# One repeating order in place of three: a software-pipelined kernel without order strings of its own for start and end

## The reference

```python
x = L0(x, theta, phi)                   # rotate pairs of the 256 columns by two angles of the sequence
# L1, expert chosen by the sequence: 256 -> 1024 -> 256, gelu between
y = layernorm(gelu(x @ Wi[e] + bi[e]) @ Wo[e] + bo[e] + x) * gamma[e] + beta[e]
# L2, one of three branches chosen by the sequence, two of them with two matmuls, the third with three
y = layernorm(y + branch_c(y)) * gamma + beta
# L3, conditioned transformer layer, 16 heads of 16
x = layernorm(y) * (1 + scale) + shift
q, k, v = x @ Wq + bq, x @ Wk + bk, x @ Wv + bv
p = softmax(q @ k.T / 4 + bias[b, h], masked)     # bias is 32 x 16 x 256 x 256
x = x + (p @ v) @ Wo + bo
h = layernorm(x) * g2 + beta2
out = x + gelu2(h @ W1 + b1) @ W2 + b2            # 256 -> 1024 -> 256
```

## Time and profile before

| | |
|---|---|
| median of 3 runs | 2104.13 us (2099.43 to 2105.55) |
| the profiled execution, its own time | 2105.55 us |
| span in its profile | 2103.8 us |
| mean granted TensorE clock | 0.985 |
| PE busy | 1934.4 us, 92% |
| DVE busy | 1591.0 us, 76% |
| ACT busy | 1377.0 us, 65%, of which 437.5 us are 341 table loads |
| DMA | 356 MB, mean 169 GB/s |

### The profile page before, as it was taken

The page is one execution under the profiler, slowest core; times in us unless marked ns, Lnnn a source line. Parts: engine busy times, 40 slices in busy tenths (PEclk is TensorE's granted clock), DMA queues, the critical chain, the costliest instruction groups (busy, mean ns, idle before and its releaser), DMA issues.

```text
span 2103.8 us, 43391 instructions
## 1 busy us (share of the span) xinstructions
PE 1934.4 (92%) x14131; PEld 1678.5 (80%) x14354; DVE 1591.0 (76%) x5373; ACT 1377.0 (65%) x2210; POOL 252.6 (12%) x361
## 2 busy tenths in 40 slices
PE   5789999999999999999999999999999999899786
PEld 4678888888888888888888888888888888788676
DVE  4567877777887788887777788777888877877764
ACT  3367677677667677767767767766676676666443
POOL 1111111011111011111101111101111110111100
PEclk9799999999999999999999999999999999999998
DMA  6656555665555465654555655556665545653350
GB/s 207 206 155 181 184 151 155 183 200 180 183 174 148 151 200 187 195 179 150 153 180 181 192 174 173 158 169 197 186 194 183 174 145 166 213 156 130 117 151 11
DMA packets 222311, 356.12 MB, mean 169 GB/s; under 512 B 29523, under 2 KB 120147, under 8 KB 222068
## 3 DMA queue, kind: packets, MB, share of 16 engines
q1 hardware_dynamic: 222068, 352.99, 54.7%
HBM read 294.12 MB, written 58.79 MB: 168 GB/s over the span
## 4 chain that ended last, share of the span: by engine, by line
PE 68%; DVE 20%; issue 7%; ACT 3%; DMA 1%; ACTq 0%; SPq 0%; POOL 0%; DVEq 0%; POOLq 0%
PE pD L471 44%; PE pX L687 12%; PE pS L471 10%; DVE bias_ring L1178 8%; DVE bias_ring L975 5%; PE pC L471 1%; PE pC L709 1%; DVE x_nat L972 1%; DVE crossed L972 1%; ACT L777 1%; ACT gelu_out L777 1%; ACT probs L777 1%; DMA out<-res 1%; ACT hid L777 1%; DVE y_nat L978 0%
## 5 line engine op out<-in xcount | busy, mean ns | idle before, releaser
L1178 DVE CUSTOM_DVE_ANT_0 bias_ring<-pS,bias_ring 128x256 f32<-128x256 f32 x1024 | 389.6, 418 | 221.8 <-PE pS L471 219.9
L777 ACT ACTIVATE probs<-pX 128x512 f32<-128x512 f32 x512 | 304.6, 595 | 249.8 <-PE pX L687 247.8
L777 ACT ACT_TABLE_LOAD x341 | 437.5, 1283 | 19.5 <-PE pD L471 12.0
L687 PE MATMUL pX<-ident,bias_ring 128*128 128x128 f32 x2048 | 326.8, 283 | 91.0 <-DVE bias_ring L975 73.8
L687 PEld LDWEIGHTS pX<-ident,bias_ring 128*128 128x128 f32 x2048 | 229.0, 142 | 191.2 <-DVE bias_ring L975 181.2
L975 DVE TENSOR_SCALAR bias_ring<-bias_ring,row_max 128x256 f32<-128x256 f32 x1024 | 321.4, 356 | 18.3
L471 PE MATMUL pS<-k_stack,q_stack 96*128 96x256 f32 x1024 | 305.1, 380 | 0.9 <-DMA k_stack<-k_spill 0.9
L471 PE MATMUL pD<-x,raw 128*128 128x256 f32 x1024 | 248.3, 386 | 1.8 <-ACT gelu_out L777 1.0
L471 PE MATMUL pD<-raw,gelu_out 128*128 128x256 f32 x1024 | 238.2, 380 | 0.0
L471 PEld LDWEIGHTS pS<-k_stack,q_stack 96*128 96x128 f32 x1024 | 198.3, 194 | 20.1
L471 PEld LDWEIGHTS pD<-x,raw 128*128 128x128 f32 x1024 | 189.3, 192 | 27.2 <-issue 4.1
(11 more groups left out here) (148 smaller groups left out, 3700.5 us busy)
## 6 DMA issues: line engine op xcount, KB each, us to landing
bias_ring<-in_fside SPq DMA_DIRECT2D x512, 256.0 KB, 4.2
raw<-in_experts SPq DMA_DIRECT2D x128, 512.0 KB, 4.6
q_spill<-hid SPq DMA_DIRECT2D x96, 256.0 KB, 3.4
k_spill<-hid SPq DMA_DIRECT2D x96, 256.0 KB, 3.4
q_stack<-q_spill SPq DMA_DIRECT2D x128, 192.0 KB, 4.0
k_stack<-k_spill SPq DMA_DIRECT2D x64, 384.0 KB, 5.6
norm<-in_expert_rows SPq DMA_DIRECT2D x32, 384.0 KB, 4.0
x_nat<-in_x SPq DMA_DIRECT2D x32, 256.0 KB, 3.3
```

The costliest lines, as they stand in the source:

```text
L687: last = e.transpose(pX[:, k, t * P:(t + 1) * P], bias_ring[:, u % NBIAS, t, k * P:(k + 1) * P], ident[:, :])
L777: return e.activation(o, i, func, bias=bias, scale=scale)
L1178: e.tensor_tensor_reduce(bias_ring[:, n, t, :], pS[:, t, :], bias_ring[:, n, t, :], 1.0, -3.4e38, ALU.add, ALU.max, row_max[:, n, t:t + 1] ...
```

## The change

FIRST and LAST go. The repeating string runs 36 times, and each engine leaves out the first letters of f, h and r, as many as SKIP says; letters of a stream that has ended do nothing.

```diff
-FIRST = {...}
-LAST = {...}
-OUTSIDE = 7
+SKIP = {"PE": (9, 101, 37), "ACT": (14, 56, 55), "DVE": (12, 53, 47), "POOL": (3, 0, 6), "SP": (10, 42, 4)}
...
+            skip = dict(zip("fhr", SKIP[engine]))
             next(extra, None)
-            for letter in FIRST[engine] + ORDER[engine] * (NB - OUTSIDE) + LAST[engine]:
-                next(streams[letter], None)
+            for _ in range(NB + 4):
+                for letter in ORDER[engine]:
+                    if skip.get(letter):
+                        skip[letter] -= 1
+                    else:
+                        next(streams[letter], None)
```

More of the change, by code:

```diff
@@ L30 @@
 MASKED = -2.0 ** 100
[L36 to L49, removed]
 ORDER = {
```

## The result

| | before | after |
|---|---|---|
| median | 2104.1 us (2099.43 to 2105.55) | 2119.64 us (2117.53 to 2122.37) |
| profiled execution, span in it | 2105.55, 2103.8 | 2116.27, 2114.5 |
| mean granted TensorE clock | 0.985 | 0.980 |

The changed kernel is slower: ratio 1.0079, 95% interval 1.0058 to 1.0099. The forecast was 2102.3, with a range to 2117. What these two traces show is therefore some two thirds of the loss; the traces of the experiments account for the rest (at the end of the account of the prediction).

The account below looks back on a forecast made before the run. PE was taken to bound the middle (busy 1481 of 1550.5 us), unchanged, but not the ends. Start +2.1 and end -3.9 gave -1.8 us: span 2102.0, or 2102.3 against the median 2104.1; range 2092 to 2117.

Parts of the forecast that it names:

- What does not change: Middle, repetitions 5 to 29: same order and distances as before, so its 1550.5 us stay.
- The start, g1's turn: Start: DVE's rotation, moved ahead of f0's first sum, ends at 56.4; PE turns at 58.2 without waiting, 2.3 us gained.
- The serial part: Start, ahead of h0: g1 ends at 78.3, then uncovered f0 and f1 steps; h0's first turn at 110.7, was 89.4.
- h0, 16 cycles ... 56.7: Start, h0's heads: 52.2 us by cycles, plus 3 for DVE's block and 1.5 for small waits, to 167.4.
- DVE has f1's sum and scaling between maxima 1 and 2, 3 us more: Start, inside h0: this DVE block adds 3 us to the cycles.
- The start's sum of +2.1: Whole start: its end comes at 259.6 us against 257.5, a loss of 2.1 us.
- Repetition 32: End, no g left: 51.2 us by cycles, +4.4 for DVE and +0.9 for clock, 56.5; old stretch 57.8.
- Repetition 33 ... 46.6 by cycles, 50.3 taken: End, r alone and f31 v: 46.6 us by cycles, 50.3 taken because the old 49.1 had exceeded its rule.
- The 23.0 and 36.4: Last stretches: h31 turn 7 to 15 takes 23.0 us (24.8 before), then r31 alone 36.4 (36.9 before).
- Bunched r steps and the clock: Slower rival at the end: bare cycles at half clock, ten to twelve, cost +10 us, 2112; chance 0.13.
- The serial start: Slower rival: f0 q, k, v and f1 lose g1's cover, up to +14 us at the start, 2114; chance 0.17.

Follow-up runs that it names:

- j: Kernel before with the repeating order at the end and extra unread transposes in bare cycles of the last 24 heads and r31's waits: 2103.03 us, 0.9996.
- l: Kernel before, old order throughout, with extra unread transposes in the last 24 heads and in r31's waits: 2107.76 us, ratio 1.0013.
- o: Changed kernel with f1's sum and scaling moved on DVE ahead of h0's maxima 0 and 1: 2119.56 us, ratio 1.0066.
- a: Changed kernel's new start with the old LAST at the end: 2117.75 us, ratio to before 1.0061.
- k: Changed kernel, order untouched, with the transposes of h at the start and of j at the end: 2109.55 us, ratio to before 1.0019.
- h: Changed kernel with 80 extra unread transposes on PE ahead of waits of f0 and f1: 2116.74 us, ratio to before 1.0054.
- b: Kernel before with old FIRST kept and the repeating order to the end: 2110.57 us, ratio 1.0023.
- d: Kernel before with all of g1 ahead of f0's q, k and v, then the old order and LAST: 2125.47 us, ratio 1.0099.
- i: Kernel before with 48 extra unread transposes ahead of the first matmul and 38 in f0's waits: 2103.4 us, ratio 0.9999.
- r: Old start with the transposes of i, repeating order at the end with those of j: 2100.79 us, ratio to before 0.9977.
- g: Kernel before with the repeating order until h30 turn 6, then the old order of what is left, no transposes: 2106.57 us, ratio 1.0007.

## Why the prediction was wrong, by its steps

- **What does not change** held: 1550.8 for 1550.5 us, and 31.3 and 60.8 for the 31.5 and 60.7 ahead of it. ACT has one table load more (342 for 341, 1.3 us each), which the prediction did not have.
- **The start, g1's turn**: 58.2 as forecast, but by luck. The rotation was done at 53.6 and not 56.4, because the input had landed by 51.4, and PE did not wait for it. PE itself came late, busy without a gap at half clock (a clock of 0.50 from 50 us on):

```profile
51.43 0.76 DVE L943 TENSOR_TENSOR crossed<-x_nat,rot_sin 128x256 f32<-128x256 f32 x2 [5.61 <-DMA x_nat<-in_x]
```

```profile
58.13 1.09 PE L442 MATMUL pD<-ident,x_nat 128*128 128x128 f32 x4
```

  In j and l, with the old start, g1 turn came at 58.2 and 58.1 as well, so the 2.3 us that were forecast as gained are inside what chance does there.
- **The serial part** was right: g1 done at about 79 (78.3), h0 turn 0 at 112.3 (110.7), and q_stack and k_stack did not hold it up.
- **"h0, 16 cycles ... 56.7"** is the step that failed at the start: 61.6. "DVE has f1's sum and scaling between maxima 1 and 2, 3 us more" was not what was short: it cost 2.1 (4.4 for 6.5 in o), and the three cycles with two g steps took 15.2 us for the 16.1 they were given. The nine cycles of 2.6 (turns 0, 4 to 8 and 12 to 14) took 28.5 us for 23.4: four were 2.6, the others 3.3 to 4.7. The three cycles of the deep branch took 4.4, 5.5 and 5.2, together 15.0 for 12.8. I priced cycles by PE's steps; DVE's and ACT's steps of the same sequences stand in some of them. For turn 5 that is DVE's scaling of g2, shown above; in turns 10 and 11 PE waits 1.4 us for DVE and 2.0 for ACT inside the deep branch, and these two cycles were there to be read in the trace of before (h0 turns 14 and 15, 5.4 and 5.2 us). These waits were read in the trace, not tried; the one block that was tried, in o, gave 2.1 us in its cycle and nothing in the time.
- **The start's sum of +2.1** was +8.5 in the trace, and 0.61%, 12.8 us, in a's time. By the ladder below, 8.8 us of the loss are order.
- **Repetition 32**: 56.7 for 56.5 in the kernel after, by luck: with the same order the eight other traces have 58.3 to 60.6, at clocks of 0.94 to 0.89 in place of 0.97.
- **"Repetition 33 ... 46.6 by cycles, 50.3 taken"** failed: 53.7, and 51.6 in j_end_warm and 51.3 in k with a clock of 0.97 and 1.00. **The 23.0 and 36.4** were 24.2 and 37.6; with transposes 23.1 and 33.9 in k. The sum was 297.7 for 291.9, and 300.9 to 301.9 in the three other traces of this end. The step that failed here is the clock: 0.9 us for it in repetition 32 and nothing in the three stretches behind. Over these stretches it is some 7 us that transposes take back, and up to 4 in repetition 32 that they do not.
- **Bunched r steps and the clock**, a rival at 0.13, is what happened at the end. It was priced at 10 us. The transposes took 7.2 us from h's median and 7.5 from b's (0.35% and 0.27% by the ratios, 7.4 and 5.7 us); in the traces of the end they took 7.7 and 7.2. The page TensorE: Matmul & The Clock Gate of the Trainium skill, cited there, agrees in kind: the clock over the last 37.6 us was 0.76.
- **The serial start**, a rival at 0.17, had its price nearly right (+10 to +14), but its point of decision, h0 turn 0 after 117, was wrong: it came at 112.3 and the loss was there. d shows the same from the other side.
- **The two rivals together** were not given a chance. With b's loss alone the kernel stays inside the range, with a's alone it is at its upper edge (2116.9 by the ratio); their sum, 2104.1 + 12.8 + 4.8 = 2121.7 by the ratios of a and b, does not.

The ladder, each step one edit: after 1.0079; transposes at the start 1.0054; and at the end 1.0019; the old order of the start 0.9977. In time that is 2119.6, 2116.7, 2109.6, 2100.8: 2.9 us clock at the start, 7.2 clock at the end, 8.8 the order of the start (the last rung also has i's 86 transposes there in place of h's 80). By the ratios the three steps are 5.3, 7.4 and 8.8 us, so the first is the least certain. The last rung lies under the kernel before, 2.2 us of it between j and r by transposes in the old start. That these gained nothing between before and i leaves open how much of it is the clock.

Why the medians of after and before differ by 4.8 us more than their traces can be read from the other traces. Up to h27 turn 7 six of them have the start of before, and they reach it between 1803.7 and 1809.0 us, on average at 1806.0; before, at 1808.0, is the second slowest. The two with the start of after reach it at 1816.8 (after) and 1815.9 (a): 10.3 us later on average, and not 8.8. From there on after was the fastest of the four traces of its end, whose mean is 300.6 us, against 296.2 for the five of the old end: 4.4, and not 1.9. Together that is 14.7 us, near the 15.5 of the medians. The profiled execution of before had a poor start, and that of after a good end.

## What to carry to other kernels

Price a reordered stretch on every engine, cycle by cycle: a cycle that is bare on PE may hold another engine's block, and work moved ahead of the heads is repaid only if the heads then get shorter. Where the steady order is cut off into a ramp, look at the granted clock of the ramp beside its idle time; here an end with cycles in which PE is busy 1.0 of 2.6 us lost some 7 us to the clock alone. Matmuls without use in such waits brought that back, and the same ones put into the old end, on top of its work, cost 3.6 us. And trace a kernel more than once before a stretch of a few microseconds is explained: one order's end varied by 4 us here.

## What the hardware showed that was not expected

- The same cycle of matmuls without a wait inside took 6.0 us at a clock of 0.53 and 3.7 at 1.00. A bare head cycle, PE's turn and scores and then DVE's maximum and subtraction, lost less: 3.4 us at 0.53 (h0 turn 0 before) and 2.6 at 1.00 (after).
- The tail of one chain, r31 alone, took 33.9 us at a clock of 1.00 (k), 35.0 at 0.93 (j), 37.6 at 0.76 (after), 36.9 at 0.86 before.
- Six traces have the start of before without a change (before, b, g, j, l, m). g1 turn came between 58.1 and 60.5 us in them, and h27 turn 7 between 1803.7 and 1809.0: 5.3 us of chance in one trace, more than most edits here.
- Between 2000 and 2077 us in the kernel after the clock fell to a mean of 0.90 and 0.93 though PE never stood longer than 2.2 us at a time.
